# A state-space stack on one core: PE's side work stood over to other places of a group, and four times three matmuls that nothing reads

## What is computed

```python
def _ssm_layer(x, A_log, Dp, W_dbc, W_dt, b_dt):
    A = -jnp.exp(A_log)
    dbc = jnp.einsum('ble,ce->blc', x, W_dbc)
    delta, Bm, Cm = jnp.split(dbc, [DT_RANK, DT_RANK + N_STATE], axis=-1)
    delta = jax.nn.softplus(jnp.einsum('blr,er->ble', delta, W_dt) + b_dt)
    dA = jnp.exp(delta[..., None] * A)
    dBx = (delta * x)[..., None] * Bm[:, :, None, :]
    ...
    _, hs = jax.lax.associative_scan(combine, (dA, dBx), axis=1)
    y = jnp.einsum('blen,bln->ble', hs, Cm)
    return y + Dp * x
```

## Time and profile before

| | |
|---|---|
| median of 3 runs | 6769.01 us (6760.99 to 6769.22) |
| the profiled execution | 6773.74 us, span 6771.6 us |
| mean granted TensorE clock | 0.852 |
| DVE busy | 6079.0 us (90%) |
| POOL busy | 5857.8 us (87%) |
| PE matmul busy | 5095.6 us (75%) |
| ACT busy | 4964.5 us (73%) |
| DMA engines, mean busy share | 0.7 in most slices |

### The profile page before, as it was taken

The page is one execution under the profiler, slowest core; times in us unless marked ns, Lnnn a source line. Parts: engine busy times, 40 slices in busy tenths (PEclk is TensorE's granted clock), DMA queues, the critical chain, the costliest instruction groups (busy, mean ns, idle before and its releaser), DMA issues. The chain is left out here.

```text
span 6771.6 us, 112630 instructions
## 1 busy us (share of the span) xinstructions
PE 5095.6 (75%) x34128; PEld 2061.5 (30%) x34128; DVE 6079.0 (90%) x3973; ACT 4964.5 (73%) x10234; POOL 5857.8 (87%) x932
## 2 busy tenths in 40 slices
PE   6777777777777777777777777777777777775787
PEld 2233233233333323323332222223223222222344
DVE  7999999999999999999999999999999999996543
ACT  6777777778777787787777777777777877874121
POOL 7999999999999999999999998999999999994211
PEclk8888888888888888888888888888888888986888
DMA  6777777777777777777777777777777878874000
GB/s 230 253 252 257 254 257 255 250 254 250 250 253 252 251 259 259 253 255 254 248 250 253 251 244 242 249 242 250 240 251 245 260 257 265 261 253 147 5 7 7
DMA packets 560031, 1561.74 MB, mean 231 GB/s; under 512 B 171954, under 2 KB 318002, under 8 KB 559730
## 3 DMA queue, kind: packets, MB, share of 16 engines
q1 hardware_dynamic: 559858, 1559.96, 70.1%
HBM read 1469.03 MB, written 90.59 MB: 230 GB/s over the span
## 5 line engine op out<-in xcount | busy, mean ns | idle before, releaser
L650 POOL TENSOR_TENSOR u<-u,Bt 128x2976 f32<-128x2976 f32 x896 | 5786.2, 6489 | 393.8 <-DMA u<-dx_rows 392.4
L615 DVE TENSOR_TENSOR_SCAN hT<-decay,u 128x744 f32<-128x744 f32 x3584 | 5799.0, 1682 | 330.0 <-ACT decay L453 307.4
L453 ACT ACTIVATE decay<-decay,a_neg 128x371 f32<-128x371 f32 (+2 forms) x7168 | 3606.2, 556 | 846.7 <-PE decay L296 775.1
L296 PE MATMUL decay<-stk,spread 96*128 96x371 bf16 (+2 forms) x7168 | 1995.0, 368 | 1471.0 <-DVE hT L615 1393.0
L314 PE MATMUL z_bank<-hT,Cst 128*32 128x256 f32 x21504 | 1744.7, 451 | 5.5 <-DVE hT L615 3.0
L296 PEld LDWEIGHTS decay<-stk,spread 96*128 96x128 bf16 x7168 | 458.9, 102 | 3094.0 <-DVE hT L615 2653.9
L462 ACT COPY z_sb<-z_bank 128x512 f32<-128x512 f32 x1344 | 798.6, 594 | 444.1 <-PE z_bank L314 432.4
L314 PEld LDWEIGHTS z_bank<-hT,Cst 128*32 128x32 f32 x21504 | 625.3, 122 | 876.3 <-issue 619.9
L1082 POOL TENSOR_TENSOR wr<-pr 128x744 f32<-128x744 f32 x8 | 14.1, 1759 | 397.2 <-DVE pr L1005 397.2
L385 PEld LDWEIGHTS prep_bank<-tmap,yT 64*128 64x128 f32 x1344 | 223.5, 244 | 105.8 <-issue 105.8
L385 PE MATMUL prep_bank<-tmap,yT 64*128 64x32 f32 (+3 forms) x1344 | 251.0, 329 | 0.0
(11 more groups left out here) (163 smaller groups left out, 2579.4 us busy)
## 6 DMA issues: line engine op xcount, KB each, us to landing
u<-dx_rows SPq DMA_DIRECT2D x3584, 372.0 KB, 4.5
delta_parts<-parts SPq DMA_DIRECT2D x112, 279.0 KB, 8.0
stk<-delta_parts SPq DMA_DIRECT2D x112, 279.0 KB, 5.1
y_rows<-z_sb SPq DMA_DIRECT2D x1792, 12.0 KB
yT<-y_rows SPq DMA_DIRECT2D x112, 192.0 KB, 6.8
dx_rows<-dx SPq DMA_DIRECT2D x112, 186.0 KB, 4.7
xT<-in_x SPq DMA_DIRECT2D x64, 186.0 KB, 5.2
xP<-in_x SPq DMA_DIRECT2D x64, 186.0 KB, 4.1
```

The lines of the kernel that those rows point to most:

```text
L296: nc.tensor.matmul(slot[:, e, :, 1:], spread[0:PARTS * QR, TILES_G * q + er // TILES_G, :], src[:, er % TILES_G, :, 1:], start=True, stop= ...
L453: last = nc.scalar.activation(bank, bank, ACT.Exp, scale=a_neg[:, l, c:c + 1])
L615: nc.vector.tensor_tensor_scan(hT[q % 2][:, i * PAIR:(i + 1) * PAIR], pair_slot(p), u[c % RING][:, part * PAIR:(part + 1) * PAIR], 0.0, AL ...
L650: tt(here, here, Bt[buf][:, :].unsqueeze(1).broadcast_to([P, 2 * HALVES * CHUNK, W0]), ALU.mult).then_inc(s_u, 1)
```

## The change

Five things, all inside the layers:

1. On PE, `to_channels` becomes `times_D` (place 23) and `to_channels` in three parts (25, 27, 29) of two blocks each. The items move from 1, 19, 23 to 0, 17, 19, the third sum from 8 to 9, the second `take_off` from 16 to 15.
2. `keep_busy` is new: at places 8, 16 and 24, and at place 1 where there is a group before, three matmuls with the operands of a spread (96 rows, 372 columns, bfloat16) into `zb`, the bank of the contraction, at a time when it holds nothing. Nothing reads them; the next fill overwrites them.
3. On ACT, t_v is gone: the absolute value and the relu read the dt product from PSUM with scale and bias of their own. The relu now counts as the read of that bank. Middle, low, B and C stand two to five places earlier, `post` at 29.
4. On SP, the 16 stores of y rows stand after chunks 10 to 14 (3, 4, 3, 3, 3), `load_yT` after chunk 15.
5. The semaphore relu_done is gone.

```diff
-                    if 9 <= c < 13 and prev:
-                        for t in range(4 * (c - 9), 4 * (c - 8)):
+                    if 10 <= c < 15 and prev:
+                        for t in range((0, 3, 7, 10, 13)[c - 10], (3, 7, 10, 13, 16)[c - 10]):
                             diagonal(prev, 1 - half, t)
...
-                    if c == 14 and prev:
+                    if c == 15 and prev:
                         load_yT(prev)
...
+            def keep_busy(at, buf, q):
+
+                if q or not known_below(G(at), 1):
+                    pe.wait_ge(s_zev, FILLS * (TILES_G * G(at) + q))
+                for _ in range(3):
+                    nc.tensor.matmul(zb[:, 0:W0], spread[0:PARTS * QR, 0, :], stk[buf][0:PARTS * QR, 0, :],
+                                     start=True, stop=True)
...
-                    if after and p in (1, 19, 23):
-                        item(after, 1 - half, (1, 19, 23).index(p))
-                    if after and p in (5, 7, 8):
-                        sum_delta(after, (5, 7, 8).index(p))
-                    if after and p in (13, 16):
-                        take_off(after, (13, 16).index(p))
-                    if prev and p in (27, 29):
-                        to_channels(prev, after, (27, 29).index(p))
+                    if p in (8, 16, 24) or p == 1 and prev:
+                        keep_busy(here, half, -1 if p == 1 else q - 1)
+                    if after and p in (0, 17, 19):
+                        item(after, 1 - half, (0, 17, 19).index(p))
+                    if after and p in (5, 7, 9):
+                        sum_delta(after, (5, 7, 9).index(p))
+                    if after and p in (13, 15):
+                        take_off(after, (13, 15).index(p))
+                    if prev and p == 23:
+                        times_D(prev, after)
+                    if prev and p in (25, 27, 29):
+                        to_channels(prev, (25, 27, 29).index(p))
...
+            def absolute(at):
                 l, _ = at
-                n = G(at)
-
-                act.wait_ge(s_item, 3 * n + 1)
+                act.wait_ge(s_item, 3 * G(at) + 1)
                 sc, bi = cols[:, 2 * l:2 * l + 1], cols[:, 2 * l + 1:2 * l + 2]
-                nc.scalar.activation(t_v[:, :], prep[:, 0:W0], ACT.Identity, scale=sc, bias=bi).then_inc(s_read, 1)
+                nc.scalar.activation(t_abs[:, :], prep[:, 0:W0], ACT.Abs, scale=sc, bias=bi).then_inc(s_abs, 1)
...
-                    if prev and p == 31:
+                    if prev and p == 29:
                         post(prev)
```

More of the change, by code:

```diff
@@ L90, in ssm_stage @@
         y_out = sb("y_out", [P, W0])
-        t_v, t_abs, t_w = [sb(n, [P, W0]) for n in ("t_v", "t_abs", "t_w")]
+        t_abs, t_w = [sb(n, [P, W0]) for n in ("t_abs", "t_w")]
         t_one, t_ln, t_relu, delta, dx = [sb(n, [P, W0]) for n in ("t_one", "t_ln", "t_relu", "delta", "dx")]
@@ L364, in take_off, with times_D, to_channels @@
                 last.then_inc((s_rest, s_rest2)[i], 1)
-            def to_channels(at, after, part):
+            def times_D(at, after):
+                l, _ = at
+                pe.wait_ge(s_xP, 16 * (G(at) + 1))
+                if after:
+                    pe.wait_ge(s_read, 3 * (G(after) + 1))
+                if pair_mean[l]:
+                    x = xP[:, :].rearrange("p (t two) -> p two t", two=2)
+                    nc.tensor.matmul(prep[:, 0:W0 // 2], d_diag[:, l, :], x[:, 0, :], start=True, stop=False)
+                    nc.tensor.matmul(prep[:, 0:W0 // 2], d_diag[:, l, :], x[:, 1, :], start=False, stop=False)
+                else:
+                    nc.tensor.matmul(prep[:, 0:W0], d_diag[:, l, :], xP[:, :], start=True, stop=False)
+            def to_channels(at, part):
                 l, _ = at
@@ L371, in to_channels @@
                     pe.wait_ge(s_yT, 16 * (n + 1))
[L372 to L380, removed]
                 w = CG * TB // 2 if pair_mean[l] else CG * TB
                 base = 0 if pair_mean[l] else CG * TB
-                for k in (range(2) if part == 0 else range(2, KB)):
+                for k in range(2 * part, 2 * part + 2):
                     m = w if k < KB - 1 else (W0 - CG * TB * (KB - 1)) * w // (CG * TB)
@@ L386, in to_channels @@
                                             start=False, stop=(k == KB - 1))
-                if part == 1:
+                if part == 2:
                     last.then_inc(s_Y, 1)
@@ L418, in _ @@
                 fill(LAST, 1, TILES_G - 1, i)
-            to_channels(LAST, None, 0)
-            to_channels(LAST, None, 1)
+            times_D(LAST, None)
+            for i in range(3):
+                to_channels(LAST, i)
         @block.scalar
@@ L489, in take_C @@
                     ins.then_inc(s_read, 1)
-            def absolute(at):
-                act.wait_ge(s_read, 3 * G(at) + 1)
-                nc.scalar.activation(t_abs[:, :], t_v[:, :], ACT.Abs).then_inc(s_abs, 1)
             def decayed(at):
@@ L507, in logarithm @@
                 nc.scalar.activation(t_ln[:, :], t_w[:, :], ACT.Ln, bias=1.0).then_inc(s_ln, 1)
-            def positive(at):
-                act.wait_ge(s_read, 3 * G(at) + 1)
-                nc.scalar.activation(t_relu[:, :], t_v[:, :], ACT.Relu).then_inc(s_relu, 1)
             def high(at):
@@ L561, in body @@
                         high(after)
+                    if p == 13:
+                        middle(after)
                     if p == 15:
-                        middle(after)
+                        low(after)
                     if p == 17:
-                        low(after)
-                    if p == 21:
                         take_B(after, 1 - half)
-                    if p in (24, 25):
-                        take_C(after, 1 - half, p - 24)
+                    if p in (19, 21):
+                        take_C(after, 1 - half, (19, 21).index(p))
             first = (0, 0)
-            take_dt(first)
             absolute(first)
+            positive(first)
             decayed(first)
@@ L576, in _ @@
             logarithm(first)
-            positive(first)
             high(first)
```

17 lines of the change are left out of this document (11 added, 6 removed).

## The result

The changed kernel took 6548.23 us (median of 4 runs, 6545.2 to 6549.64) beside 6769.11 us (6760.99 to 6777.38) of the kernel before on the same chip: a ratio of 0.9673, 95% interval 0.9656 to 0.969. That is 3.3% faster; the forecast was 6556.

The account below looks back on a forecast made before the run. VectorE, idle 307.4 us for ACT's decays, was taken as the bound, at most 355 us to be had. From 6773.7, 187 (group's end) and 26 (loop) off gave 6561, as median 6556 us; 8 in 10 range 6465 to 6660.

Parts of the forecast that it names:

- the likeliest case: The forecast itself: clock up at the end of half the groups and half the loop's surplus gone, 6556 us; 70%.
- The floor: VectorE's group without waits: 32 scans of 1.603 us plus 0.43 for dx, 51.73 us.
- (1): PE's new order at places 23 to 29: 1.97 or 1.37 us a group, middle 1.67, 187 us in all.
- (2): Added matmuls at 1, 8, 16, 24: nothing at 8 to 24; the 0.67 us loss at the group's start stays.
- (3): ACT's dt Identity dropped: ACT isn't late at those places, so no gain except half a microsecond in the first group.
- (4): Layer 1's loop: ACT's stall behind the branch costs 1.6 us a group; half of 52 gained, 26 us.
- (5): SP's later row stores and yT load: 0.9 us late at worst, within the slack of 1.7; no effect.
- the fourth rival: The yT load comes late and PE waits before place 25's y part; at 12 us landing, 6914 us; 4%.
- POOL did not take over: Rival in which POOL, at 55.2 us a group with its idle time, becomes the bound: 6769 us, no gain; 3%.
- the forecast's own range: From half way to the first rival, 6489 us, to the second's order gain without the loop, 6640.
- the two rules weighed: PE's clock: the skill says long idle gaps bring it down; the trace shows a fall with longest wait 1.5 us.
- The second rival: The clock falls all the same, added matmuls do nothing; only the order gains 1.37 a group: 6683 us; 15%.

Follow-up runs that it names:

- e3: The changed kernel with six added matmuls at place 24 and none at 1, 8 and 16; 6447.83 us, 0.9545 of the kernel before.
- e1: The changed kernel without the twelve added matmuls of a group; 6569.04 us, 0.9723 of the kernel before.
- e9: e1 with the dt product back at place 1 and ACT's absolute value and relu behind decay 1; 6684.21 us, 0.9871 of the kernel before.
- e4: The changed kernel without the three added matmuls at place 1, those at 8, 16 and 24 kept; 6481.97 us, 0.9601 of the kernel before.
- e6: The changed kernel with t_v kept on ACT (Identity over dt, absolute value and relu read it); 6591.02 us, 0.9738 of the kernel before.
- e7: The kernel before with only ACT's code shifted by already satisfied waits in the last groups of layers 0 and 1; 6727.21 us, 0.9941.
- e5: The changed kernel with SP's old list (stores after chunks 9 to 12, yT load after 14); 6546.82 us, 0.9674 of the kernel before.
- e11: The changed kernel with three added matmuls at place 24 and none elsewhere; 6486.54 us, 0.9581 of the kernel before.
- e10: The kernel before, old order, with six added matmuls at place 24 and none elsewhere; 6578.77 us, 0.9723 of the kernel before.
- e8: e3 with ACT's code shifted by 48 waits in the last groups of layers 0 and 1; 6446.13 us, 0.9524 of the kernel before.

## Why the prediction was right

The forecast of 6556 us was 8 too high, and the likeliest case is the one that came. Its terms, with what the runs put in their place:

- **The floor and where the waits are: right.** 51.92 us for a group without waits against 51.73, and 220 of the 224.5 us are VectorE's waits for decays.
- **(1) The end of a group: right in kind, 28 us too much.** The waits at 28 and 29 are gone, and in layer 0 the clock is up in every second group, as assumed: of the loop's 60 groups all had the low clock somewhere in places 24 to 27 before, 30 have it after (and 8 in e3). But a group at half clock loses 0.99 + 0.1 at place 31, not 0.6: I counted the queue only up to place 29, and PE is still behind at 31. With half the groups at 1.09 the gain is 1.97 - 0.55 = 1.42 a group, 159 us against 187.
- **(2) The added matmuls: the step that failed.** At 8, 16 and 24 they cost nothing, right. "That keeps the 0.67 us of places 2 and 3" gave nearly the right size by two errors. I put the clock of the group's start in the sum but not the new order there, which takes those waits away by itself (e1 has none at 2 and 3 in layer 0; in e9 they are back). The three matmuls at place 1 then return 49 us of it (e4). What stayed is 0.78 + 0.1 in half the groups, 0.44 against 0.67: a gain of 26 us that isn't in the sum.
- **(3) ACT's t_v: nothing, right for layers 0 and 2, though not for the reason given.** "ACT isn't late at those places" held in the old order; with the dt product behind spread 0 it is late there once t_v is kept, by 0.55 us a group, but the group as a whole doesn't get longer (e6). The 44 us that e6 costs are layer 1's loop stall and belong to (4).
- **(4) The loop: right in place, half was too little.** From dx to dx, layer 1's groups took 56.2 us on average against 54.6 in layer 0, a surplus of 1.67; after, 53.07 against 52.89. That is 1.49 x 32 = 47 us of 53, not 26. The reason that I gave first, y_out leaving its place before the branch, is not enough: e6 has y_out at 29 too, and its layer 1 lost 47 us. The code is still fetched in every round (e7); why ACT stands still for it in the kernel before and in e6, and hardly in the change, is open.
- **(5) SP: nothing, right** (e5). The load of yT landed within 6.3 us at most, and the fourth rival had no ground. PE waits for it once, 13.3 us behind the last group, as before (14.8). POOL did not take over: its idle time fell by 225 us.

With the measured terms: 159 + 26 + 47 = 232 us against 224.5 of the span; the forecast had 213. The misses of (1) and of (2) and (4) have opposite signs, 28 us too much and 47 too little, so that the total came within 8 us is in part luck. The upper end of the forecast's own range, 6640, doesn't follow from its terms either, which give 6769 - 153 = 6616.

On the clock the trace decides between the two rules weighed. The Trainium skill ("TensorE: Matmul & The Clock Gate", section "Why this matters for your kernels") speaks of long idle gaps. One of the two falls agrees in kind: in e3 it follows PE's wait of 2.71 us at place 0. The other does not: in the kernel before no wait at the lull was over 1.5 us. PE's own longest idle time at places 18 to 25 was 1.11 us in every group, as here, ahead of the spread in which the clock of the earlier trace rows falls:

```profile
3025.60 0.68 PE L296 MATMUL decay<-stk,spread 96*128 96x371 bf16 x2 [1.11 <-DVE hT L615]
```

And three matmuls at place 24 save 96 us (e11), six in the old order 2.8% (e10). The second rival, in which the added matmuls do nothing for the clock, falls with that.

Open: how much work at place 24 holds the clock in every group (e11's mean is 0.892, e3's 0.921, and their times 0.0036 apart); what is left at place 1 and in the first groups; what the dt product's new place is worth without ACT's new order; and which position of ACT's code stalls a loop, since only one shift was tried in the kernel before.

## What to carry to other kernels

Where an engine works an ordered list, first find the places without slack (here 0 and 1, where 32 places don't divide by three slots) and price every operation at them and directly behind them; where PE waits anyway, added matmuls cost nothing that can be told. Heavy work behind a lull on PE can run at half clock: look at the granted clock where the heavy part starts, and if it has fallen, try cheap work in the lull just ahead. A change that mixes such edits should be split before it is kept: here one quarter of the added matmuls brought the gain and another quarter gave half of it back. And a difference between two runs should be split by stage before it is explained: e6's 44 us look like 0.4 us in each of 112 groups, with waits in the trace to match, and lie in one layer alone.

## What the runs showed of the hardware

- Matmuls that nothing reads made the kernel faster: six per group at one place raised the mean granted clock from 0.852 to 0.92 and took 2.8% off the time in the old order (e10), and PE's busy time fell though it had more to do, from 5095.6 to 4857.3 us. Three per group ahead of a place without slack cost 49 us (e4).
- The clock does not fall at once. In e3 PE was idle for a whole 2 us window with a granted clock of 1.00; in the next it was 0.79, and in the one after 0.50, with PE busy again. And it falls without a long gap: in the kernel before PE was never idle for over 1.11 us at a time at places 18 to 25, and in layer 0 the clock fell behind them in each of the loop's 60 groups.
- 36 instructions without effect, outside the loops, took 42 us off the kernel before (e7), and the 8192-byte instruction transfers within layer 1's loop, 35 in 800 us, were gone: where ACT's loop lies in its code was worth 0.6%. Fetches alone are no loss: e3 had 36 of them in the same stretch and e8 none, at the same time within the intervals.
